# Preparing the second layer's first batch inside the first, ScalarE's copies of projection pairs, and earlier norms

## What is computed

```python
# x (8, 2048, 256) fp32, adj (2048, 2048), symmetric, with ones on the diagonal
h = jnp.maximum(_layernorm(x, axis=-1), 0.0)
x = x + _L0_gnn_ref(h, adj, ...)       # masked attention, 4 heads
h = jnp.maximum(_layernorm(x, axis=-1), 0.0)
x = x + _L1_gnn_ref(h, adj, ...)       # graph attention, 4 heads

# _L1_gnn_ref
Wh = jnp.einsum('bnf,hfd->bhnd', x, W)
ei = jnp.einsum('bhnd,hd->bhn', Wh, a1)
ej = jnp.einsum('bhnd,hd->bhn', Wh, a2)
e = ei[:, :, :, None] + ej[:, :, None, :]
e = jnp.where(e > 0, e, ALPHA * e)
e = jnp.where(adj[None, None] > 0, e, MASK_VAL)
att = jax.nn.softmax(e, axis=-1)
h = jnp.einsum('bhij,bhjd->bhid', att, Wh)
# ... heads side by side, then jax.nn.elu(h)
```

## Time and profile before

| | |
|---|---|
| median of 3 runs | 4523.58 us (4523.34 to 4524.16) |
| the profiled execution | 4522.35 us, its span 4520.6 us |
| TensorE busy | 4328.3 us, 96% of the span |
| VectorE busy | 3414.3 us, 76% |
| ScalarE busy | 2977.7 us, 66% |
| GpSimd busy | 3109.9 us, 69% |
| layer 0 until its last product | 0 to 2856.6 us |
| first instruction of layer 1 | 2860.06 us |
| first matmul of `work` | 2950.69 us |

### The profile page before, as it was taken

The page is one execution under the profiler, slowest core; times in us unless marked ns, Lnnn a source line. Parts: engine busy times, 40 slices in busy tenths (PEclk is TensorE's granted clock), DMA queues, the critical chain, the costliest instruction groups (busy, mean ns, idle before and its releaser), DMA issues. The chain is left out here.

```text
span 4520.6 us, 83340 instructions
## 1 busy us (share of the span) xinstructions
PE 4328.3 (96%) x34312; PEld 2531.1 (56%) x34312; DVE 3414.3 (76%) x4242; ACT 2977.7 (66%) x3498; POOL 3109.9 (69%) x2262
## 2 busy tenths in 40 slices
PE   7999999999999999999999999399999999999997
PEld 3334334334334334333333333299999999999997
DVE  4875875776776776776687677388888988889885
ACT  3664664664665665566566466188888888878885
POOL 4685685675675676676577477367787868778785
PEclk9999999999999999999999999699999999999999
DMA  6001001001001000000000000111120212212111
GB/s 200 10 10 38 10 10 30 19 10 29 20 10 29 20 10 28 20 8 27 15 10 20 10 10 20 54 34 55 48 83 27 76 33 71 67 38 81 32 57 43
DMA packets 126973, 160.82 MB, mean 36 GB/s; under 512 B 8833, under 2 KB 109185, under 8 KB 126593
## 3 DMA queue, kind: packets, MB, share of 16 engines
q1 hardware_dynamic: 126592, 155.49, 11.0%
...
## 5 line engine op out<-in xcount | busy, mean ns | idle before, releaser
L585 ACT ACTIVATE e_sb<-e_sb 128x1024 f32<-128x1024 f32 x1024 | 1081.2, 1057 | 898.2 <-DVE e_sb L687 861.2
L687 DVE SCALAR_TENSOR_TENSOR e_sb<-psS,mask 128x1024 f32<-128x1024 f32 x1024 | 1202.7, 1216 | 436.5 <-PE psS L816 435.9
L1426 PE MATMUL psA<-xy,ring_p 128*128 128x195 bf16 x8192 | 1398.1, 248 | 9.7 <-DVE red L1303 9.7
L1426 PE MATMUL psA<-xy,ring_s 128*128 128x195 bf16 x8192 | 1397.8, 248 | 0.0
L418 POOL TENSOR_TENSOR e_sum<-e_sb 128x1024 f32<-128x1024 f32 x384 | 918.5, 2392 | 463.1 <-ACT e_sb L585 331.5
L1222 ACT ACTIVATE ring_s<-eiB,ejb 128x1024 int8<-128x1024 f32 x1024 | 1088.5, 1135 | 9.9 <-PE psA L1426 9.9
L816 PE MATMUL psS<-qT,kT 64*128 64x512 f32 x4096 | 1020.0, 616 | 4.6 <-DVE e_sb L687 4.5
L829 PE MATMUL psN<-e_sb,v_sb 128*32 128x512 f32 x8192 | 985.2, 598 | 12.5 <-ACT num L523 12.5
L1426 PEld LDWEIGHTS psA<-xy,ring_p 128*128 128x128 fp8e4 x8192 | 799.3, 98 | 13.7 <-DVE red L1303 11.5
L1426 PEld LDWEIGHTS psA<-xy,ring_s 128*128 128x128 fp8e4 x8192 | 798.4, 97 | 7.9
L816 PEld LDWEIGHTS psS<-qT,kT 64*128 64x128 f32 x4096 | 351.7, 186 | 642.4 <-issue 404.8
...
## 6 DMA issues: line engine op xcount, KB each, us to landing
...
```

The costliest lines, as they stand in the source:

```text
L585: act.activation(e_sb[:, n % ES], e_sb[:, n % ES], ACT.Exp, scale=SCALE).then_inc(exp_done, 1)
L687: dve.scalar_tensor_tensor(out=e_sb[:, n % ES], in0=psS[:, s % 2], scalar=-CLIP_RAW, in1=mask[:, kb, cols][:, None, :].to_broadcast([P, 2, ...
L1426: ins = pe.matmul(psA[:, i % BANKS, br * PARTS * XW:(br + 1) * PARTS * XW], part[:, n % RING, k, tt * TW + j * P:tt * TW + (j + 1) * P], x ...
```

## The change

The state that both layers need moves into an object (`Between`), whose tensors and semaphores both get. `layer0` now also does what `layer1` did ahead of its slot 0:

- The gap before the last batch has 8 more groups (`GAPX`). In it SP loads the four tiles of batch 0's x1 over the `xin` tiles as they come free, VectorE takes their norms at v = 6, 10, 14 and 18, and from v = 18 on TensorE transposes them into `psN` and `psD` and projects them into `psS`; ScalarE copies the transposes, ScalarE and VectorE the projections. The terms of batch 0 follow in groups 6 to 41 of the last batch. The scores of the last batch wait for all copies.
- The loads of W and a, and W a1 and W a2 (`weights`), come in the first batch; the reduction of the mask to one bit (`one_bit_masks`) is the last thing on VectorE in layer 0.

In `layer1`, slots begin at g = -17 instead of -84. For batch 1 the tiles stand at -2 + 10 t. `H_AT1` is -1 instead of 1: four slots, not two, from the norm to the transposes. ScalarE copies both banks of a projection pair in one instruction, and VectorE none.

```diff
-def layer0(nc, mask, x, adjT, wqT, wkT, wvT, woT, bq, bk, bv, bo, gamma, beta, x1, nb):
...
+H_AT1, TR_AT1, HT_AT1, WH_AT1, COPY_AT1 = -1, 3, 5, (7, 11), (9, 13)
...
+GAPX = 8
+NORM1_AT, TURN1_AT, WH1_AT = (6, 10, 14, 18), (18, 19, 23, 27), (19, 23, 27, 31)
+RS1_AT, EJ1_AT, EIT1_AT, CEN1_AT, EXP1_AT, XQV1_AT = (6, 7, 8, 9), 22, 35, 38, 40, 41
+WALL_AT = 2
...
+        xin = wh[:, :, :, :].rearrange("p k h e -> p (k h e)")[:, 0:BLK * F].rearrange("p (t j f) -> p t j f", t=T, j=TB)
...
+            before = k + GROUPS + gap(b - 1)
+            return [(b, k)] + ([(b - 1, before)] if b and before < TAILG else [])
+        def gap(b):
+            return GAPG + (GAPX if b == nb - 2 else 0)
...
+                    if t == T - 2 and b + 2 == nb:
+                        for i in range(2):
+                            sp.wait_ge(x1_out[i], T // 2 * 16)
+                        for u in range(T):
+                            sp.wait_ge(tr_done, (nb - 1) * T + u + 1)
+                            if u >= 2:
+                                sp.wait_ge(h1_done, u - 1)
+                            sp.dma_start(xin[:, u], tile_of(x1_v, 0, u)).then_inc(x1_in[u % 2], 16)
+                    if t == 0 and b + 1 == nb:
+                        exchange_max()
...
+            sp.wait_ge(ei_out, 16 * BLK)
...
+            def second_layer(v):
+                for t in range(T):
+                    if v == TURN1_AT[t] + (1 if t else 0):
+                        act.wait_ge(tr1_done, t + 1)
+                        act.activation(hT[:, t % 2, 0], psN[:, :], ACT.Copy)
+                        act.activation(hT[:, t % 2, 1], psD[:, :], ACT.Copy).then_inc(hT1_done, 1)
+                    for i in range(2):
+                        if v == WH1_AT[t] + 1 + i:
+                            act.wait_ge(wh_proj, 2 * t + i + 1)
+                            act.activation(wh[:, TB * t + 2 * i].rearrange("p h e -> p (h e)"),
+                                           psS[:, i, 0, 0:H * W1], ACT.Copy).then_inc(wh_done[0], 1)
...
+            def weights():
+                dve.wait_ge(w_in, 64)
+                wlink = linker(dve, w_chain, 0)
+                for c in range(FH):
+                    for part in range(2):
+                        wlink(dve.tensor_tensor(wa, w_all[:, c, :, 0:D], a_rows[:, part], ALU.mult))
+                        wlink(dve.tensor_reduce(w_all[:, c, :, D + part], wa, AX.X, ALU.add))
+            def second_layer(v):
+                for t in range(T):
+                    if v == NORM1_AT[t]:
+                        dve.wait_ge(x1_in[t % 2], 16 * (t // 2 + 1))
+                        ln_moments(dve, link, mv1[:, TB * t:TB * t + TB], stats, tmp1[:, 0:TB], lambda j: xin[:, t, j, :], TB)
+                        for j in range(TB):
+                            ins = dve.tensor_scalar(xin[:, t, j, :], xin[:, t, j, :], mv1[:, TB * t + j, 0:1], 0.0,
+                                                    ALU.subtract, ALU.max)
+                        ins.then_inc(h1_done, 1)
+                    for i in range(2):
+                        if v == WH1_AT[t] + 1 + i:
+                            dve.wait_ge(wh_proj, 2 * t + i + 1)
+                            dve.tensor_copy(wh[:, TB * t + 2 * i + 1].rearrange("p h e -> p (h e)"),
+                                            psS[:, i, 1, 0:H * W1]).then_inc(wh_done[1], 1)
...
+            def one_bit_masks():
+                dve.wait_ge(edge_done, 1)
+                for k in range(0, BLK, 4):
+                    dve.tensor_tensor(adj_w[:, k:k + 4], adj_w[:, k:k + 4],
+                                      edge_w[:, :, None].to_broadcast([P, 4, N // 4]), ALU.bitwise_and)
...
+                    if b == 0 and k == WALL_AT:
+                        weights()
+            dve.memset(edge[:, :], EDGE).then_inc(edge_done, 1)
+            one_bit_masks()
...
+                if s == 0 and b == nb - 1:
+                    for i in range(2):
+                        pe.wait_ge(wh_done[i], 2 * T)
...
+            def second_layer(v):
+                for t in range(T):
+                    for i in range(2):
+                        if v == WH1_AT[t] + i:
+                            if i == 0:
+                                pe.wait_ge(hT1_done, t + 1)
+                            if t:
+                                for k in range(2):
+                                    pe.wait_ge(wh_done[k], 2 * (t - 1) + i + 1)
+                            elif i:
+                                pe.wait_ge(v_done, nb * (BLK // 2))
+                            else:
+                                pe.wait_ge(q_done, nb * (T * PAIRS))
+                            for k in range(2):
+                                nodes = slice((2 * i + k) * P, (2 * i + k + 1) * P)
+                                ins = product(psS[:, i, k, 0:H * W1], lambda c: hT[:, t % 2, c, nodes],
+                                              lambda c: w_all[:, c].rearrange("p h e -> p (h e)"))
+                            ins.then_inc(wh_proj, 1)
+                for t in range(T):
+                    if v == TURN1_AT[t]:
+                        pe.wait_ge(h1_done, t + 1)
+                        if t == 0:
+                            pe.wait_ge(numcopy_done, (nb - 1) * GROUPS)
+                            pe.wait_ge(sums_read, (nb - 1) * HALVES)
+                        for c in range(FH):
+                            for j in range(TB):
+                                ins = pe.transpose((psN, psD)[c][:, j * P:(j + 1) * P], xin[:, t, j, c * P:(c + 1) * P], ident[:, :])
+                        ins.then_inc(tr1_done, 1)
...
-H_AT1, TR_AT1, HT_AT1, WH_AT1, COPY_AT1 = 1, 3, 5, (7, 11), (9, 13)
...
-        FIRST, LAST = PREP_FROM - SLOTS, nb * SLOTS + 24
+        FIRST, LAST = MULT_W[0] - SLOTS - 1, nb * SLOTS + 24
 
         def preparing(g):
-            return [(b, g - SLOTS * (b - 1)) for b in range(nb) if PREP_FROM <= g - SLOTS * (b - 1) < SLOTS]
+            return [(b, g - SLOTS * (b - 1)) for b in range(1, nb) if PREP_FROM <= g - SLOTS * (b - 1) < SLOTS]
...
-            return [(b, (s - LN0 - at) // LN_STEP) for b, s in preparing(g)
-                    if 0 <= s - LN0 - at < T * LN_STEP and (s - LN0 - at) % LN_STEP == 0]
+            found = []
+            for b, s in preparing(g):
+                first, step = (-2, 10) if b == 1 else (LN0, LN_STEP)
+                if 0 <= s - first - at < T * step and (s - first - at) % step == 0:
+                    found.append((b, (s - first - at) // step))
+            return found
...
-                        act.activation(wh[:, b % 2, TB * t + 2 * i].rearrange("p h e -> p (h e)"),
-                                       psP[:, 0, 0:H * W1], ACT.Copy).then_inc(wh_done[0], 1)
+                        act.activation(whs[b % 2][:, TB * t + 2 * i:TB * t + 2 * i + 2].rearrange("p k h e -> p k (h e)"),
+                                       psP[:, :, 0:H * W1], ACT.Copy).then_inc(wh_done[0], 1)
...
-            dve.memset(edge[:, :], EDGE).then_inc(edge_done, 1)
-            dve.wait_ge(edge_done, 1)
-            for k in range(0, BLK, 4):
-                ins = dve.tensor_tensor(adj_w[:, k:k + 4], adj_w[:, k:k + 4],
-                                        edge_w[:, :, None].to_broadcast([P, 4, N // 4]), ALU.bitwise_and)
-            ins.then_inc(adj_done, 1)
-            dve.wait_ge(const_in, 64)
-            link = linker(dve, w_chain, 0)
-            for c in range(FH):
-                for part in range(2):
-                    link(dve.tensor_tensor(xf[:, 1, 0:H, 0:D], w_all[:, c, :, 0:D],
-                                           xf[:, 0, part * H:part * H + H, 0:D], ALU.mult))
-                    ins = dve.tensor_reduce(w_all[:, c, :, D + part], xf[:, 1, 0:H, 0:D], AX.X, ALU.add)
-                    link(ins)
-            dve.wait_ge(adj_done, 1)
...
-                for i in range(2):
-                    for b, t in tile_at(g, COPY_AT1[i]):
-                        pair = (b * T + t) * 2 + i
-                        dve.wait_ge(wh_proj, pair + 1)
-                        if t == 0 and i == 0 and b >= 2:
-                            dve.wait_ge(xf_done, (b - 1) * (2 * H))
-                        dve.tensor_copy(wh[:, b % 2, TB * t + 2 * i + 1].rearrange("p h e -> p (h e)"),
-                                        psP[:, 1, 0:H * W1]).then_inc(wh_done[1], 1)
```

291 lines of the change are left out of this document (188 added, 103 removed).

## The result

The changed kernel takes 4510.16 us (median of 13 runs, 4506.14 to 4519.52), the kernel before 4523.58 (13 runs, 4522.03 to 4527.56). The ratio is 0.9973, with a 95% interval of 0.9966 to 0.998: 13 us faster, where 51 were forecast. 4510 lies outside the range of 4457 to 4491, so the prediction was wrong in size, right in sign. The profiled execution took 4509.78 us, span 4508.0; the working's own sum for it was 4471.5, or a span of 4469.7. The miss to explain is 38.3 us of span.

What follows compares the result with a forecast made beforehand. TensorE was taken as the bound, its work unchanged, so only its idle time could be won. Terms +21.5 + 8 - 68.2 + 1.8 - 14 = -50.9 us gave 4471.5 profiled, about 4472 median; range 4457 to 4491.

Steps and rivals of the forecast that it cites:

- A: Gap before batch 7, first layer: added transposes and projections make it longer, +21.5 us (bounds 18.7 and 30).
- B: Tail of the first layer: masks on VectorE hold up GpSimd's chain of 16 operations, +8 us (bounds 0 and 9).
- C: Start of the second layer: its first batch comes already prepared, -68.2 us.
- D: Later batches of the second layer: most of TensorE's 3.06 us wait per batch goes, -14 us (bounds -20 and 0).
- The 0.2 us for the rest: First layer: allowance for W's small operations in batch 0 and the terms in batch 7, since VectorE mostly waits there.
- Rival 2: First layer's tail: GpSimd isn't held by the masks or its chain slips through, time 4464 us; chance 0.15.
- I let it come to the fourth piece at +30.5: Second layer's start: TensorE reaches the fourth piece of masks 30.5 us after the weighting starts (bounds +28 and +34.2).
- What comes last then?: Second layer's later batches, stall removed: the reduction behind the norm comes last, with 1 us to spare.
- The boundary in question: Tile boundary before the second tile's transposes at 3364.87: reduction needed at 3352.3, first part ready at 3351.4.
- I take a third off for this.: Later batches: gain of 18.4 + 1.2 us cut to 14, as one GpSimd clash of about 2 us would use up the spare.
- Rival 1: Second layer's batches: the stall only changes its name, TensorE waiting for reductions instead of the copy; time 4486 us, chance 0.2.
- Rival 4: Second layer: norms ahead of reductions make TensorE wait in all 28 norm groups; slower than before, 4570 at 3 us each; chance 0.03.

Runs made afterwards that it cites:

- e7: The changed kernel with the norm behind the reduction and the products of W moved from the first batch's group 2 into the preparation: 4465.79 us.
- e11: Against e7, only VectorE's pieces 1 to 9 of the second layer's first batch placed one to four slots later: 4465.8 us.
- e1: The changed kernel with H_AT1 set back from -1 to 1, so the norm stands two slots ahead of the transposes: 4496.15 us.
- e3: The changed kernel with the norm in the same slot, but written behind that slot's reduction instead of in front of it: 4469.28 us.
- e8: Against e7, the four mask operations also moved from the first layer's tail to the head of VectorE's second-layer program: 4465.85 us.

## Why the prediction was wrong, point by point

The span before was 4520.6 and the sum -50.9; the span after is 4508.0, 38.3 us more. The misses of the terms, each by its own stretch, come to 38.0: A +4.0, B -0.1, C +8.0, D +26.1.

**What bounds the kernel.** Right: TensorE's work didn't change, and all that was won or lost is its idle time.

**A, the gap: nearly right in the gap, mis-sized outside it.** The gap went from 51.65 us (2467.04 to 2518.69) to 75.27 (2469.29 to 2544.56). Without the 3.8 us of the output projection that is +19.8, for some 21.3. The 0.2 us for the rest failed: the products of W made turn 7 come 2.25 us late, and the terms of batch 0 cost 3.4 us between groups 14 and 41 of batch 7. VectorE does wait for TensorE in most groups there, but for at most 2.4 us at a time, and 6.1 us of products in one group are more than that. e7 gave the first part back, 2.2 us of span. The last aggregate of the layer came at 2870.33 instead of 2844.79: +25.5 for +21.5. (The bound of 30 isn't its own sum: 18.7 and eight times 0.6 and four times 1.3 are 28.7.)

**B, the masks in the tail: right.** VectorE's and GpSimd's timelines in the tail, which answer to the earlier trace rows:

```profile
2870.33 0.38 DVE L884 BATCH_NORM_AGGREGATE cq<-cq 128x2 f32<-128x6 f32 x4
...
2870.76 8.90 DVE L938 TENSOR_TENSOR mask<-mask,edge 128x2048 int32<-128x2048 int32 x4
...
2870.79 2.35 POOL L101 TENSOR_SCALAR cq<-cq 128x4 f32<-128x4 f32 x1 [2.86 <-DVE cq L884]
2873.22 2.09 POOL L102 TENSOR_SCALAR cq<-cq 128x4 int32<-128x4 int32 x1
2875.39 2.12 POOL L104 TENSOR_TENSOR cq<-cq 128x4 f32<-128x4 f32 x1
2877.60 2.12 POOL L105 TENSOR_TENSOR cq<-cq 128x4 f32<-128x4 f32 x1
2879.81 0.19 POOL L106 TENSOR_SCALAR cq<-cq 128x4 f32<-128x4 f32 x1
```

Four operations of 2.1 to 2.35 us and twelve of 0.2: from the aggregate to the chain's end 12.8 us instead of 4.9, +7.9 for +8. One row of 2.25 us at another place of the kernel was enough for it, and the rule of the Trainium skill that was cited with it (SBUF — State Buffer, "Who interferes with whom") agrees with these rows. Rival 2 falls. The same mechanism then decided term D, where the prediction gave it a third of 20 us.

**C, the start: right up to the first matmul, 8 us short behind it.** The first instruction of the layer is the weighting, and `work` starts 14.2 us behind it (2893.48 to 2907.66), where 14.0 were forecast for its last input. The transposes ahead of slot 2 wait, as forecast, and run cold (1.97 us for 1.06). TensorE came to the fourth piece at +30.1, for "I let it come to the fourth piece at +30.5". The step that failed is that nothing was priced behind it: VectorE's first reductions stand in its program behind pieces whose signs don't exist yet, 8 slots ahead. The reduction that slot 4.5 needs ran at 2930.03, behind two pieces that took 4.6 and 4.1 us. That wait (2.82 us), 1.07 us at slot 8.5 (behind batch 1's second norm, with 3.61 us of subtractions), and 2.37 at slot 56.5 (the mechanism of D) are 6.3 us of the miss. Behind the first of them the granted clock is 0.83 over 10 us, as in the stretch that cost 1.65 us; that is most of the rest (an estimate from that stretch). The forecast asked what the fourth piece waits for and not what waits behind it. e11 put the reductions ahead of the pieces and won nothing, so the order on VectorE isn't all of the cause; that ScalarE's signs are the rest wasn't shown by a run.

**D, the stall: wrong in sign, and two thirds of the miss.** Forecast -14 (bounds -20 and 0), measured +12.1 (1172.9 to 1185.0). Where the stall came from was read rightly: "It waits for VectorE's copy, and that stands behind a norm", and the norm is the cause (e1). Its cost was read too small: with the clock behind it, what was to be had is not 18.4 + 1.2 us but the 24.8 that e3 wins. The step that failed is the answer to "What comes last then?": one boundary with 1 us to spare, where two others have none.
- *The boundary in question.* One was worked out, the reduction of slot 3. That one is as forecast: in batch 2 the norm ahead of it took 5.0 us (a clash of 2 us, 3.18 us of subtractions), the reduction began at 3327.35, and TensorE didn't wait. But all four norms, in slots 55, 3, 15 and 27, now stand ahead of the reduction of their slot. The one at 27 met nothing (1.14 us of subtractions in batch 1, and its reduction waited for TensorE). Those at 15 and 55 weren't priced, and they are the ones with 7.2 us against the cover of 1.35 to 3.2 us.
- *"I take a third off for this."* A share of the gain can't bound a cost that falls at other places. Three waits, 5.4 us together, stand in a batch where one of 3.06 was, and behind four of the eleven waits of over 2 us in batches 1 to 6 the clock cost 1.6 us more.

Rival 1 named this mechanism at a chance of 0.2, with D = 0 as its price, since a stall that changes its name was thought to cost what it had cost. It costs more, being three waits for one. The end of the range, 4491, lies only 5 us above its 4486. Rival 4 had the place as well, but 28 groups at 3 us were too many: batches 1 to 6 have 17 waits of 0.9 to 2.4 us, and 11 of them are directly behind a norm. The bound of 0 on D had no row behind it. A norm that can take 9 us (1.4 and 0.3 of statistics and the 7.30 of the earlier trace rows) and a cover of 1.35 to 3.2 us, side by side, would have given 6 us or more at a boundary; rival 4 has these two numbers, and term D doesn't use them. D put the norm in at 3.0 us, as if the 7.30 belonged to the place that it left. GpSimd is busy 150 of 196 us, and at the new places the four subtractions took 5.4, 3.2, 5.4 and 1.1 us (slots 55, 3, 15 and 27).

With the norm behind the reduction (e3) the same change takes 4469.28 us, 3 us from the forecast. That nearness is luck: by the same stretches its terms miss by +3.9 (A), -0.1 (B), +4.2 (C) and -10.8 (D). With the products of W in the preparation it takes 4465.79 us (e7), 0.9869 of the kernel before (0.9855 to 0.9884); of all versions that ran, this and its equals e8 and e11 are the fastest.
